# Self-attention's last maxima on TensorE: eleven steps instead of sixteen parts in the group next to the last

## What is computed

```python
q = (x @ wq).reshape(B, T, H, D)               # T = 2048, H = 16 heads, D = 16
lat = x @ w_down
k = (lat @ wk_up).reshape(B, T, H, D)
v = (lat @ wv_up).reshape(B, T, H, D)
q = _apply_rope(q, cos, sin)
k = _apply_rope(k, cos, sin)
scores = jnp.einsum('bqhd,bkhd->bhqk', q, k) * scale
pages = jnp.arange(T) // PAGE_SIZE             # pages of 64 tokens
allowed = pages[None, :] <= pages[:, None]
scores = jnp.where(allowed[None, None], scores, jnp.finfo(scores.dtype).min)
attn = jax.nn.softmax(scores, axis=-1)
out = jnp.einsum('bhqk,bkhd->bqhd', attn, v).reshape(B, T, E)
return out @ wo
```

## Time and profile before

| | |
|---|---|
| runs | 813.0, 813.98, 814.86 us |
| profiled execution | 815.49 us, span of its instructions 813.6 us |
| mean granted clock of TensorE | 0.962 |
| TensorE busy | 753.8 us, 93% of the span |
| VectorE busy | 620.8 us, 76% |
| ScalarE busy | 427.2 us, 53% |
| self-attention's groups | about 78 to 531 us of the span |
| group (3, 2) with the units of (3, 3) | 456.4 to 495.6 us |
| group (3, 3) | 499.5 to 531 us |

### The profile page before, as it was taken

One profiled execution on the slowest core, in us unless ns is written; L12 is line 12 of the kernel. 1 busy time (PEld: TensorE's weight loads), 2 busy tenths in 40 slices (PEclk: granted clock), 3 DMA queues, 4 the chain that ended last, 5 costly groups with the idle time before them and its releaser, 6 DMA issues. The chain is left out here.

```text
span 813.6 us, 12188 instructions
## 1 busy us (share of the span) xinstructions
PE 753.8 (93%) x4329; PEld 394.8 (49%) x4329; DVE 620.8 (76%) x1107; ACT 427.2 (53%) x879; POOL 150.2 (18%) x170
## 2 busy tenths in 40 slices
PE   7874897999999999999999997989999999999997
PEld 5431232333223333223333331268658888888886
DVE  4899687888998889999888762037736777787885
ACT  1453263676667776666777875932133333333353
POOL 2555000000000000000000000003314555555520
PEclk9997698899999999999999998999999999999999
DMA  7598341020000000000180000030002122222103
GB/s 211 166 254 257 54 118 40 1 67 27 27 2 2 0 2 1 1 1 1 48 254 2 1 1 2 1 114 1 0 1 78 56 70 81 81 81 81 40 1 104
DMA packets 27152, 47.32 MB, mean 58 GB/s; under 512 B 6112, under 2 KB 23008, under 8 KB 26336
## 3 DMA queue, kind: packets, MB, share of 16 engines
q1 hardware_dynamic: 25184, 43.94, 18.0%
q10 hardware_dynamic: 1920, 2.75, 1.2%
HBM read 38.16 MB, written 8.39 MB: 57 GB/s over the span
## 5 line engine op out<-in xcount | busy, mean ns | idle before, releaser
L495 DVE TENSOR_REDUCE part_max<-psum 128x1 f32<-128x512 f32 (+3 forms) x560 | 341.3, 668 | 54.6 <-PE psum L681 49.5
L600 ACT ACTIVATE probs<-psum 128x512 f32<-128x512 f32 (+3 forms) x640 | 293.7, 539 | 154.9 <-PE psum L706 153.9
L681 PE MATMUL psum<-k_stack,q_stack 96*128 96x512 bf16 (+4 forms) x640 | 214.8, 364 | 18.8 <-DVE psum L481 11.5
L706 PE MATMUL psum<-q_stack,k_stack 98*128 98x512 bf16 (+4 forms) x640 | 202.2, 357 | 13.4 <-DMA q_stack<-shift 11.6
L718 PE MATMUL psum<-probs,v_all 128*17 128x512 f32 (+3 forms) x1280 | 149.1, 538 | 0.3
L681 PEld LDWEIGHTS psum<-k_stack,q_stack 96*128 96x128 bf16 (+1 forms) x640 | 60.1, 99 | 171.6 <-DVE part_max L495 120.9
L706 PEld LDWEIGHTS psum<-q_stack,k_stack 98*128 98x128 bf16 (+1 forms) x640 | 60.9, 99 | 94.4 <-ACT probs L600 39.0
L889 POOL MEMSET eps<- 128x4 f32 x1 | 0.1, 102 | 459.0 <-POOLq L282 459.0
L1501 PE MATMUL psum<-ctx_part,qc_part 128*128 128x512 f32 (+1 forms) x384 | 82.9, 366 | 1.8 <-PEq L874 1.8
L1577 PE MATMUL psum<-v_parts,p_part 128*128 128x512 f32 (+3 forms) x416 | 77.3, 342 | 0.0
L1501 PEld LDWEIGHTS psum<-ctx_part,qc_part 128*128 128x128 f32 x384 | 66.3, 189 | 14.5 <-issue 2.6
(11 more groups left out here) (145 smaller groups left out, 689.2 us busy)
## 6 DMA issues: line engine op xcount, KB each, us to landing
mask<-in_mask SPq DMA_DIRECT2D x16, 800.5 KB, 4.3
pieces<-k_stack SPq DMA_DIRECT2D x24, 256.0 KB, 4.7
q_stack<-pieces SPq DMA_DIRECT2D x24, 256.0 KB, 4.3
k_stack<-pieces SPq DMA_DIRECT2D x24, 256.0 KB, 4.7
x_sb<-in_x SPq DMA_DIRECT2D x4, 512.0 KB, 9.2
out<-x_sb SPq DMA_DIRECT2D x8, 256.0 KB, 2.2
q_stack<-in_ctxT SPq DMA_DIRECT2D x1, 1601.0 KB, 11.0
probs<-in_cos ACTq DMA_DIRECT2D x4, 256.0 KB
```

The costliest lines, as they stand in the source:

```text
L495: nc.vector.tensor_reduce(part_max[:, h:h + m, r, c:c + 1], src, axis=AX_X, op=ALU.max).then_inc(m_read, 1)
L600: nc.scalar.activation(probs[:, s % 2, h, col:BLK], s_bank[h][:, col:BLK], ACT.Exp, scale=ATTN_SCALE).then_inc(exp_done, 1)
L681: last = nc.tensor.matmul(out, q_stack[b][0:rows, g * G + h, r * P:(r + 1) * P], k_stack[c][0:rows, g * G + h, 0:keys], start=True, stop=True)
L706: nc.tensor.matmul(s_bank[h][:, col:BLK], k_stack[s // TPB][0:rows, g * G + h, (s % TPB) * P:(s % TPB + 1) * P], q_stack[b][0:rows, g * G ...
```

## The change

A constant `TURN_EARLY = 5` is added. In group (3, 2), and there alone, the sum that the entries are spread over leaves out the last five of the sixteen weights (steps 12, 13, 14, 15, and step 0 of (3, 3)): 11 x 512 = 5632 columns instead of 7424. All 39 entries are then issued by the end of step 11, and the turn stands ahead of the scores of step 12. Nothing else differs; every instruction is there as often as before, and only TensorE's order changes. Line numbers below line 110 go up by one, and by two below line 730.

```diff
--- before.py
+++ after.py
@@ -107,6 +107,7 @@
 
 
 TURN_LAG = 3
+TURN_EARLY = 5
 
 AHEAD = [(10, 10), (14, 14), (18, 18), (24, 24)]
 
@@ -726,6 +727,7 @@
                 if following(b, g):
                     pairs.append((following(b, g), 0))
                 weights = [BLK - first_col(where[0], s) for where, s in pairs]
+                reach = sum(weights[:-TURN_EARLY] if (b, g) == order[-2] else weights)
                 done = 0
                 for i, (where, s) in enumerate(pairs):
                     if s == 0:
@@ -736,11 +738,11 @@
                         pe.wait_ge(shift_sent, (index(*where) + 1) * 16 * SHIFT_ROWS)
                     for h in range(G):
                         scores(*where, s, h)
-                        due = len(entries) * (sum(weights[:i]) + weights[i] * (h + 1) / (G + 1)) // sum(weights)
+                        due = len(entries) * (sum(weights[:i]) + weights[i] * (h + 1) / (G + 1)) // reach
                         maxima(entries[done:int(due)])
                         done = max(done, int(due))
                     weigh(b, g, s - 1 if s else steps[b] - 1)
-                    due = len(entries) * sum(weights[:i + 1]) // sum(weights)
+                    due = len(entries) * sum(weights[:i + 1]) // reach
                     maxima(entries[done:due])
                     done = max(done, due)
                 if not following(b, g):
```

## The result

Four runs of each kernel: median 813.6 us before (813.0 to 814.86), 807.04 us after (805.49 to 808.25). The ratio is 0.9915, 95% interval 0.9899 to 0.993, so the kernel became 0.85% faster, some 6.6 us. 807.8 had been predicted. The profiled execution took 808.25 us, its span is 806.5.

A forecast was written before the change was run, and what follows sets the result against it. TensorE, busy 93% of the span, was taken to idle in an uncovered chain before the last group. 4.85 us there plus 1.35 from the clock made 6.2, so 807.8 us; 806.0 to 810.2 for eight in ten.

The forecast's parts named there:

- The prices of the entries: Steps 1 to 11 of (3, 2): the moved units, out and turn cost TensorE 2.45 us together.
- The turn's wait: Ahead of step 12 of (3, 2): the wait for neg_max shrinks from 1.5 to about 0.5 us.
- Steps 12 to 15: End of (3, 2): steps without moved entries take 6.2 us together, covering the chain behind the turn.
- The wait for the DMA: Scores of the last group: wait goes to zero, 4.15 us from turn to landing under 6.2 of other work.
- The clock: Start of the last group: no fall of the granted clock, gaining 1.35 us, bounds 0.9 and 1.5.
- The sum: Hand-over to the last group: 4.85 us up to its first scores plus 1.35 from the clock, 6.2 us gained.
- the later falls: Behind the last group: short clock falls may appear, vanish or change length; the sum keeps its centre, with scatter.
- rival 1: Steps 1 to 11 of (3, 2): VectorE becomes a bound and takes back 2.0 us, 809.8 us; chance 0.10.
- rival 2: Hand-over or later: clock gives less back, by 1.35 or 1 to 1.5 us; 809.2 to 809.3 us; chance 0.09.
- rival 3: Scores of the last group: shift rows still late, 1 us may stay uncovered, 808.8 us; chance 0.04.
- Rival 4: Steps 1 to 11: held units delay scores and exponentials step upon step; slower than before, 821 us; chance 0.02.

The follow-up runs named there:

- the kernel with thirteen steps: Changed kernel with TURN_EARLY = 3, entries in thirteen steps and only steps 14, 15 as cover; 808.59 us, ratio 0.9941 against the kernel before.
- the filled pause: Kernel before, with 17 products that nobody reads between the turn of (3, 3) and the wait for its shift rows; 810.81 us, ratio 0.9971.
- the turn put back: Changed kernel with the turn alone back ahead of step 0 of the last group; 811.46 us, ratio 0.9972 against the kernel before.
- the five kernels with the turn early: Changed kernel with entries in 13, 7, 9 or 12 steps, or the turn inside step 12; 808.59, 809.47, 807.74, 806.67, 807.04 us.

## Why the prediction was right

It was right in direction, place and size. Step by step:

- *The prices of the entries.* Steps 1 to 11 with what they took in and the turn's wait: predicted 2.45 + 0.5 = 2.95 us. Measured from the first product of step 1 to the first of step 12: 29.12 us before (456.41 to 485.53), 31.93 after (455.57 to 487.50), so 2.81. At three and four entries a step TensorE paid no more than the prices taken from the four-unit step. Step 1 begins with these rows, before and after:

```profile
456.41 0.39 PE L681 MATMUL psum<-k_stack,q_stack 96*128 96x512 bf16 x1
```
```profile
455.57 0.39 PE L682 MATMUL psum<-k_stack,q_stack 96*128 96x512 bf16 x1
```

- *The turn's wait.* 0.5 predicted, 0.41 measured; the last reduction ended where the sum had it (2.48 us from 484.50, against the earlier trace rows).
- *Steps 12 to 15.* 6.2 us predicted, 487.50 to 493.71 = 6.21 measured.
- *The wait for the DMA.* Gone, as predicted. The cover was larger than needed. The 4.15 us of chain had been read from the one place where it stood bare; the same chain took 3.23, 3.61 and 3.83 us in three of the experiments. The difference is the shift's DMA: it landed after 1.7, 2.1 and 2.3 us there, and after 2.6 to 2.7 in the kernel before. The earlier trace rows already had 1.7 as the median. This was the worst-sized number of the argument, and it did no harm in the forecast because any value below 6.2 gives no wait. It did mislead my expectation for the kernel with thirteen steps.
- *The clock.* 1.35 predicted, 7.64 - 6.36 = 1.28 measured, and the filled pause shows that this share stands by itself. It is not a fixed price: with the turn put back it was 7.96 - 6.36 = 1.60. ScalarE did set the pace from step 0 on, as the sum assumed: its exponentials of steps 1 to 8 follow each other without a pause from 496.60, and the new wait of 0.2 us for its copy is TensorE waiting for ScalarE.
- *The sum.* 6.2 predicted, 6.25 on the stretch: 4.97 up to the first scores (4.85 predicted) and 1.28 behind them. The medians differ by 6.6; the 0.3 beyond the stretch are within the scatter of the runs.

The rivals: VectorE is no bound at 3.55 entries (rival 1), but it is at 5.57, at its own pace. The clock stayed at full through the hand-over (rival 2). The shift rows were in time (rival 3). Rival 4 didn't show even where VectorE was the bound. Two of their sums had slips without a consequence. By rival 2's own prices (1 to 1.5 us) a longer later fall gives 808.8 to 809.3 us. Rival 3 set the 4.0 us of the earlier trace rows, from issue to landing, against 3.2 us from issue to scores; the landing in this place took 2.6 to 2.7, so turn to landing would be some 5.5 us and not 4.95, still under 6.2.

On the later falls the prediction drew on the Trainium skill (TensorE: Matmul & The Clock Gate, The HAM clock gate), which calls the observation of the clock gate free-running. The traces agree with it as far as they go. The same changed kernel, profiled twice, has its fall behind 575 us for 6.8 us in one execution (0.50 still at 580 to 582, none at 790) and for half of it in the other, which has another at 790 to 792. First execution, then second:

```profile
576.00:578.00 2.00, 2.00 (x4) 1.10 (x5) 0.59 (x5) 0.17 (x1) 1.22 (x2) 0.50 0.00 0
580.00:582.00 2.00, 2.00 (x4) 0.85 (x3) 1.98 (x2) 0.00 (x0) 1.69 (x1) 0.50 0.00 0
790.00:792.00 2.00, 1.47 (x11) 1.09 (x11) 0.95 (x4) 1.41 (x3) 0.00 (x0) 1.00 0.00 0
```
```profile
576.00:578.00 2.00, 2.00 (x4) 0.91 (x3) 1.43 (x5) 0.00 (x0) 0.54 (x1) 0.50 0.00 0
580.00:582.00 2.00, 2.00 (x12) 1.70 (x11) 1.71 (x5) 1.73 (x4) 0.56 (x1) 1.00 0.00 0
790.00:792.00 2.00, 2.00 (x10) 2.00 (x11) 1.98 (x3) 2.00 (x2) 0.00 (x0) 0.50 0.00 0
```

So these falls move between executions of one kernel, and a difference in them between two single traces says nothing about two kernels. Why they move is not shown by these traces.

## What to carry to other kernels

A short chain over several engines (a reduction, a transpose, a copy, a small DMA) costs its whole length where the work that used to cover it runs out, which is at the end of a pipeline: look there, and move the start of the chain and not its bulk. Spreading the work ahead of it more densely cost little here up to the pace of the engine that drains it; one row of a dense step elsewhere in the same trace gave that limit. When a pause is closed on TensorE, add what the clock gives back behind it, read from the same instructions at either level.

## What was not expected

**The shift's DMA has several lengths.** In the kernel before, the two transfers of the last turn landed 2.6 to 2.7 us after issue, and SyncE was busy 2.05 us with issuing them. In the changed kernel, in its repetition and in the five kernels with the turn early it was 1.7 us and 1.14 us. With the pause filled it was 2.3 us and 1.71 us, and with the turn put back 2.1 us and 1.50 us. In these three long cases a fetch of instructions (the queue q8 "instruction", 164 GB/s in one slice) came close to the issue, which begins at 496.29 us in the kernel before, and the second transfer was late. DMA rates from 496 to 500 us there, 40 slices of 0.1 us:

```profile
GB/s 0 0 0 0 0 0 0 0 0 0 164 0 0 0 18 21 0 0 0 3 0 0 0 0 0 0 0 0 0 5 29 8 0 0 0 0 0 0 0 0
```

and from 491.5 to 495.5 us in the kernel with thirteen steps, where the issue begins at 492.03 and the fetch comes behind both transfers:

```profile
GB/s 0 0 0 0 0 0 0 0 0 0 0 0 0 0 0 0 10 26 5 0 0 0 0 26 16 0 0 0 164 0 0 0 0 0 0 0 0 0 0 0
```

In the kernel before the fetch comes 0.7 us after the issue begins; with the pause filled the two coincide; with the turn put back it comes 0.2 us ahead. The six other short cases have no fetch within 3 us behind the start of the issue. That the fetch delays the second transfer fits all ten traces, but it was not tried.

**Unchanged work scatters more than the change's details.** The copy of (3, 1), ahead of which all these kernels are alike, came between 454.04 and 459.12 us in ten profiled executions, while two executions of the changed kernel agree in the hand-over stretch within 0.01 us. Where the chain is covered, versions that differ by half a microsecond can probably be ranked by such a stretch, and not by the time of the kernel. Only the changed kernel was profiled twice, so the order of the kernels with turns elsewhere rests on one trace each.
